# Masked attention on one core: the values of key group 0 as second, those of group 2 as last but one

## The reference

```python
q = x @ Wq.T + bq
k = x @ Wk.T + bk
v = x @ Wv.T + bv
scores = where(adj > 0, q @ k.T / sqrt(128), -9e15)   # 4096 x 4096, adj is int32
att = softmax(scores, axis=-1) @ v
y = x + elu(att)
out = (y - mean(y)) / sqrt(var(y) + 1e-5)             # over the 128 features
```

## Time and profile before

| what | value |
|---|---|
| median of 3 runs | 434.38 us (434.34 to 434.85) |
| the profiled execution: own time | 434.82 us |
| its span from first to last instruction | 433.0 us |
| granted TensorE clock, mean | 0.997 |
| periods 2 to 31, start to start | 13.21 us, then 12.21 to 12.42 us |
| DMA moved | 104.77 MB, mean 242 GB/s |

### The profile page before, as it was taken

The page is one execution under the profiler, slowest core; times in us unless marked ns, Lnnn a source line. Parts: engine busy times, 40 slices in busy tenths (PEclk is TensorE's granted clock), DMA queues, the critical chain, the costliest instruction groups (busy, mean ns, idle before and its releaser), DMA issues.

```text
span 433.0 us, 11489 instructions
## 1 busy us (share of the span) xinstructions
PE 419.7 (97%) x3470; PEld 309.0 (71%) x3470; DVE 361.0 (83%) x677; ACT 354.0 (82%) x742; POOL 354.2 (82%) x644
## 2 busy tenths in 40 slices
PE   7897999999999999999999999999999999999994
PEld 6653677777777777777777777777777777777784
DVE  2778899888888988888889888888888888888784
ACT  4886769888888898888888888888888988888893
POOL 0497459888988898889888988898889888898875
PEclk9999999999999999999999999999999999999998
DMA  8954999999999999999999999999999999998551
GB/s 225 383 194 82 257 260 250 238 260 272 264 253 281 259 258 245 276 271 260 245 265 272 263 242 266 275 260 251 257 275 256 249 259 284 260 255 231 102 85 39
DMA packets 149649, 104.77 MB, mean 242 GB/s; under 512 B 132738, under 2 KB 141444, under 8 KB 141444
## 3 DMA queue, kind: packets, MB, share of 16 engines
q1 hardware_dynamic: 149200, 104.41, 91.4%
q10 hardware_dynamic: 436, 0.20, 0.2%
HBM read 69.47 MB, written 2.10 MB: 165 GB/s over the span
## 4 chain that ended last, share of the span: by engine, by line
POOL 62%; issue 15%; PE 13%; ACT 4%; DVE 4%; POOLq 2%; ACTq 0%; DVEq 0%
POOL p_rows L403 29%; POOL res L417 6%; POOL neg_mean L428 4%; POOL rstd L441 4%; POOL var_eps L439 3%; POOL y L422 3%; POOL att_sum L410 3%; PE ps_out L960 3%; POOL att L412 3%; POOL centred L430 2%; POOL expm L419 2%; POOL y_out L445 2%; PE ps_scores L921 2%; PE ps_scores L922 1%; PE ps_scores L923 1%
## 5 line engine op out<-in xcount | busy, mean ns | idle before, releaser
L403 POOL TENSOR_TENSOR p_rows<-scores,p_rows 128x256 f16<-128x256 f32 x252 | 176.2, 730 | 7.2 <-ACT p_rows L560 7.2
L687 DVE CUSTOM_DVE_ANT_0 scores<-ps_scores,adj 128x1024 f32<-128x1024 f32 x128 | 156.0, 1219 | 19.6 <-issue 13.6
L543 ACT ACTIVATE scores<-scores,neg_max 128x1024 f32<-128x1024 f32 x128 | 145.7, 1138 | 3.4 <-DVE neg_max L697 3.4
L703 DVE TENSOR_TENSOR p_lo<-ps_t,p_hi 128x512 f16<-128x512 f32 x124 | 82.6, 685 | 26.4 <-ACT p_hi L552 24.5
L673 DVE TENSOR_SCALAR adj<-adj 128x1024 f32<-128x1024 int32 x128 | 99.6, 779 | 0.2 <-DMA adj<-in_adj_dram 0.2
L921 PE MATMUL ps_scores<-k_hi,q_hi 128*128 128x512 f16 x256 | 97.0, 379 | 1.9 <-DVE q_lo L654 1.6
L923 PE MATMUL ps_scores<-k_hi,q_lo 128*128 128x512 f16 x256 | 97.0, 379 | 0.0
L922 PE MATMUL ps_scores<-k_lo,q_hi 128*128 128x512 f16 x256 | 97.0, 379 | 0.0
L960 PE MATMUL ps_out<-v_parts,p_hi 128*128 128x256 f16 x496 | 95.4, 273 | 0.8 <-DVE p_lo L703 0.8
L960 PE MATMUL ps_out<-v_parts,p_turned 128*128 128x256 f16 x496 | 95.0, 273 | 0.0
L552 ACT ACTIVATE p_hi<-ps_t 128x512 f16<-128x512 f32 x122 | 71.7, 587 | 21.8 <-PE ps_t L937 18.9
(11 more groups left out here) (121 smaller groups left out, 481.9 us busy)
## 6 DMA issues: line engine op xcount, KB each, us to landing
adj<-in_adj_dram SPq DMA_DIRECT2D x64, 1024.0 KB, 5.4
out_dram<-y_out SPq DMA_DIRECT2D x32, 64.0 KB, 5.0
x_rows<-in_x_dram SPq DMA_DIRECT2D x4, 256.0 KB, 4.3
x_rows<-in_x_dram SPq DMA_DIRECT2D x2, 512.0 KB, 7.1
p_turned<-p_rows SPq DMA_TRANSPOSE x63, 4.5
w_rows<-in_L_gnn_Wq_dram ACTq DMA_DIRECT2D x1, 64.0 KB, 2.7
w_rows<-in_L_gnn_Wk_dram ACTq DMA_DIRECT2D x1, 64.0 KB, 3.3
w_rows<-in_L_gnn_Wv_dram ACTq DMA_DIRECT2D x1, 64.0 KB, 4.7
```

The lines of the kernel that those rows point to most:

```text
L403: last = nc.gpsimd.tensor_tensor(p_rows[c][:, w:][:, cols], s_sb[s][:, c * PIECE:c * PIECE + w][:, cols], p_rows[c][:, 0:w][:, cols], ALU. ...
L543: nc.scalar.activation(s_sb[s][:, cols], s_sb[s][:, cols], ACT.Exp, bias=neg_max[:, s:s + 1], accum_out=p_sums[:, s, c:c + 1]).then_inc(ex ...
L687: nc.vector.tensor_tensor_reduce(out=s_sb[s][:, cols], in0=ps_scores[c % 2][:, :], in1=mask_sb[s][:, cols], scale=SCALE, scalar=-3.0e38, o ...
L703: nc.vector.tensor_tensor(p_lo[:, k, :], ps_t[bank_of(s, g)][:, :], p_hi[:, k, :], ALU.subtract).then_inc(plo_ready, 1)
```

## The change

It swaps the places of groups in the order of the values product in every period. Group 4, the first turned group, stays first. Group 0, the first transposed group, moves from the fourth slot to the second. Turned groups 5 and 6 move back by one slot each (second to third, third to fourth). Groups 1, 7, 2 and 3 keep their slots 4 to 7. `T_AT`, and with it the place of the PE transposes and of all that ACT and DVE do, stays as it is. The tail's own order (L1026 to L1040) isn't made from `PV_ORDER` and stays.

```diff
 T_AT = {4: 6, 5: 7, 6: 8, 7: 10}
-PV_ORDER = (4, 5, 6, 0, 1, 7, 2, 3)
+PV_ORDER = (4, 0, 5, 6, 1, 7, 2, 3)
 Q_AT = (8, 9, 10, 11, 12, 13, 14)
```

## The result

The kernel after takes 430.49 us (430.16 to 431.18, 4 runs) against 434.36 us before, ratio 0.9913 with a 95% interval of 0.9900 to 0.9926. Measured again later it gave 430.63 us and 0.9921 (0.9901 to 0.9941). So 3.9 us are gained where 3.4 were forecast. To a tenth, 430.49 us is the lower end of the range given (430.5 to 432.3); the second time lies just inside it.

What follows compares the result with a forecast made beforehand. The prediction took PE to be the bound, losing time to waits for group 5's low part. Gains of 2.8 and 0.93 us less 0.3 gave 3.4, so 434.38 - 3.4 = 431.0 us, range 430.5 to 432.3.

Steps and rivals of the forecast that it cites:

- The bound and the 2.8 us: PE bounds the kernel; its slot 1 waits for group 5's low part, 2.8 us over 28 periods, all go.
- the 3.7 us in all: PE's whole loss to the wait for group 5's low part: 2.8 us in later periods plus 0.93 in period 2.
- Period 2's 0.93 us: PE's first wait for group 5's low part, in period 2: whole 0.93 us gained, 0.7 as lower end.
- The two rooms named: Period 2: group 7's transposes 1.16 us behind the low part, scores 1.17 behind a masking; both stay free by about 0.2.
- Period 6's 0.3 us: Loss taken for a new wait of PE in slot 1 of period 6, for a late transpose landing: 0.3 us.
- step 5: Period 6: transpose landing 7.4 us from issue makes slot 1 wait 0.4 us, 1.4 if issue stays, 0 if chance.
- the forecast's own range: 430.6 us (no wait in period 6, all 3.7 kept) to 431.5 us (0.7 in period 2, 0.5 in period 6).
- Rooms in every period: PE's nearest other wait, group 6's transposes on piece 3's exponential: room shrinks once from 0.56 to 0.45 us.
- Step 2: Group 5's values in slot 2: gain 2.8 us, no cost; group 7's transposes keep 1.1 us behind the low part.
- Rival A: Early gain given back at a masking in period 2 or the transpose in period 6; 432.0 us, chance 0.20.
- Rival B: Another ring of engines, not PE, sets 12.3 us, so PE's wait only moves; 434.4 us, chance 0.06.
- Rival C: Transposes land later in every period, over 7.1 us from issue, and PE waits in slot 1; 442 us, chance 0.04.

Runs made afterwards that it cites:

- new_q_banks: Kernel after with other PSUM buffers for the projections of q of groups 3 to 7 in period 1; 429.91 us.
- new_one_matmul_less: Kernel after with one of PE's 24 scores matmuls left out per period (slot 3, low part of k); 424.78 us.
- group_0_first: Kernel after with group 0 one slot earlier still, in first place ahead of group 4, in the tail too; 432.29 us.
- new_in_period_2: Kernel before with the new order in period 2 only, the old order in periods 3 to 31; 433.61 us.
- the four matmuls less: Kernel after with four scores matmuls left out per period (low part of k, groups 4 to 7); 421.07 us.
- group_2_second: Values order 4, 2, 5, 6, 0, 1, 7, 3, with group 2 in second place and its DMA transpose landing late; 518.69 us, one run.
- one matmul less: Kernel before, old order, with one scores matmul left out per period (slot 3, low part of k); 431.35 us, ratio 0.9925.

## Why the prediction was right

- **The bound and the 2.8 us.** Right. The way by period lengths gave 341.8 us for 28 periods without waits, and they took 341.79. The list of waits alone (13.3 us, period 2's among them) would have overstated the 3.7 us in all more than threefold.
- **Period 2's 0.93 us.** Right: 13.21 to 12.27 us. The two rooms named were left at 0.2 us. Order of time in the kernel after, on DVE and PE's weight loads:

```profile
44.32 0.68 DVE L703 TENSOR_TENSOR p_lo<-ps_t,p_hi 128x512 f16<-128x512 f32 x1
...
45.23 0.14 PEld L937 LDWEIGHTS ps_t<-ident,scores 128*128 128x128 f32 x1
...
48.96 1.21 DVE L687 CUSTOM_DVE_ANT_0 scores<-ps_scores,adj 128x1024 f32<-128x1024 f32 x1
...
50.41 0.10 PEld L921 LDWEIGHTS ps_scores<-k_hi,q_hi 128*128 128x128 f16 x1
```

  45.23 - 45.00 = 0.23 us, and 50.41 - 50.17 = 0.24 us.
- **Period 6's 0.3 us.** The term that was mis-sized: it was 0. The transpose landed at 92.7 us, 6.7 from issue and not 7.4, and slot 1's values began with 0.26 us to spare, at 92.96:

```profile
92.96 0.27 PE L960 MATMUL ps_out<-v_parts,p_turned 128*128 128x256 f16 x1
```

  That it was 0 is luck of the landing. The issue did move forward with PE, to 86.03 us, as step 5 said. 7.4 us from there is 93.4, which would have cost the 0.4 us that the step worked out (its 0.04 us comes from a landing at 94.95, shown rounded as 95.0). Such a wait came in other kernels with the new order, 0.25 us in new_q_banks (7.1 us to landing) and 0.63 us in new_one_matmul_less (7.4 us, and PE sooner). group_0_first had one too, with 6.7 us, as it needs the transpose a slot earlier. This 0.3 us is most of the 0.5 us between 431.0 and 430.5, and the reason why 430.49 us lies below the 430.6 from which the forecast's own range began.
- **Rooms in every period.** The exponential of piece 3 was forecast to keep 0.45 us ahead of group 6's transposes and kept 0.40 (199.32 + 1.14 to 200.86):

```profile
199.32 1.14 ACT L543 ACTIVATE scores<-scores,neg_max 128x1024 f32<-128x1024 f32 x1
...
200.86 0.14 PEld L937 LDWEIGHTS ps_t<-ident,scores 128*128 128x128 f32 x1
```

  Group 7's transposes kept 0.9 us on the low part of group 5, where 1.1 was forecast: besides the wait itself, the wait of the period before is gone too, so the low part, tied to that period, comes another 0.1 us later against PE. Step 2 counted only the one of the two. That left enough room, so the gain is as forecast.
- **Rival A** (the early gain given back) is refuted by new_in_period_2. **Rival B** (another ring sets 12.3 us): the four matmuls less put the next ring at 11.87 us. The weight-load share, one of the two measures by which the Trainium skill would judge PE's headroom (Perfetto Trace Analysis, Identifying the Most-Contended Engine), went from 71 to 73%, yet leaving out one matmul of 0.22 us shortened 27 periods by 0.22 us each. Here the trace doesn't agree with that measure: PE was the bound at 73%. The other measure, the arithmetic rate, wasn't worked out. **Rival C** (late landings) needs landings over 7.1 us from issue in every period; in the kernel after none that feeds slot 1 took more than 6.7. Its price, 0.4 us in each period, was tested by no run. group_2_second shows a larger wait that costs its whole length in each period.

## What to carry to other kernels

Where an engine is fed back to back, take its loss from the lengths of equal periods, with and without the wait, and not from the list of waits. In an in-order sequence an operand that is late by 0.1 us costs one swap with work whose operand lands well before; look then for each later reader of the late one (here the transposes that need the same buffer) and for the worst single landing, not the median. Before paying for a faster engine, check whether its wait is part of a chain that goes round over a period: here half of what one matmul less saved came back as waits. And read the granted clock wherever an engine has waited for long: in two kernels here it fell behind waits of over 2 us.

## What wasn't expected

The slow landing of the transpose that feeds slot 1 of period 6 (issued near 86 us) isn't noise alone. From issue to landing it took 6.4 to 7.9 us in every profile but that of group_2_second, where from 116 us on no transpose took over 5.9. Only its exact size was chance. Two transposes that feed slot 6 were slower still in the kernel after (9.5 us, issued at 40.4 us, and 7.3 us, issued at 54.3 us), and PE waited for neither. Why landings are slow in the early periods wasn't tried.
